# Scores in four pieces with key-projection matmuls between them, and a new order on four engines

## What is computed

```
q, k, v = split(x @ Wqkv)                      # 16 heads of 64
q, k    = l2norm(q)*qs, l2norm(k)*ks;  rotary(q, k)
out     = local_attention(q, k, v)             # windows of 32, looking one window back
x       = x + out @ Wo
x       = x + gated_gelu_ffn(layernorm(shift_tokens(x)))
```

## Time and profile before

| what | value |
|---|---|
| median of 3 runs | 1763.34 us (1762.8 to 1766.48) |
| the profiled execution's own time | 1768.14 us |
| its span in the trace | 1766.4 us |
| PE / PEld busy | 90% / 71% of the span |
| DVE / ACT / POOL busy | 77% / 72% / 73% |
| mean granted TensorE clock | 0.964 |
| the 96 `scores` groups | from 250.9 us to 1722 us, 13.5 to 19 us apart |

### The profile page before, as it was taken

One profiled execution on the slowest core, in us unless ns is written; L12 is line 12 of the kernel. 1 busy time (PEld: TensorE's weight loads), 2 busy tenths in 40 slices (PEclk: granted clock), 3 DMA queues, 4 the chain that ended last, 5 costly groups with the idle time before them and its releaser, 6 DMA issues.

```text
span 1766.4 us, 70552 instructions
## 1 busy us (share of the span) xinstructions
PE 1592.2 (90%) x29272; PEld 1260.5 (71%) x29272; DVE 1363.8 (77%) x1875; ACT 1274.8 (72%) x1888; POOL 1294.2 (73%) x1227
## 2 busy tenths in 40 slices
PE   6999968889999999999998999998989988989986
PEld 4777856667777777777776777766767766767774
DVE  5677866787887888888887878877877877877863
ACT  3788845677787778767886877777777777667663
POOL 3311168787987888888899878888877988778761
PEclk8999998999999999999999999999999999999997
DMA  5211112433334333334333343333343333333331
GB/s 150 62 47 44 44 37 63 126 87 77 94 78 107 96 86 91 86 77 128 81 94 95 77 124 81 84 83 84 76 124 72 91 81 81 72 71 77 71 75 42
DMA packets 127629, 146.51 MB, mean 83 GB/s; under 512 B 58448, under 2 KB 71504, under 8 KB 125776
## 3 DMA queue, kind: packets, MB, share of 16 engines
q1 hardware_dynamic: 127312, 141.98, 32.6%
HBM read 25.47 MB, written 1.05 MB: 15 GB/s over the span
## 4 chain that ended last, share of the span: by engine, by line
PE 70%; ACT 10%; issue 9%; DVE 4%; POOL 3%; SPq 3%; DMA 1%; ACTq 0%; POOLq 0%; DVEq 0%
PE banks L1260 41%; PE banks L1582 9%; PE banks L1542 8%; PE banks L1498 7%; PE banks L1390 4%; ACT vst L839 4%; ACT banks L854 3%; SPq L414 2%; POOL arena L631 1%; POOL arena L586 1%; POOL arena L637 1%; DMA arena<-vst 1%; DVE gq L1169 0%; DVE small L1131 0%; PE banks L1600 0%
## 5 line engine op out<-in xcount | busy, mean ns | idle before, releaser
L581 POOL TENSOR_TENSOR arena<-arena 128x1024 f32<-128x1024 f32 x96 | 230.7, 2403 | 87.8 <-DVE arena L1102 87.4
L1097 DVE TENSOR_TENSOR arena<-banks,tabs 128x1024 f32<-128x1024 f32 x192 | 233.9, 1218 | 49.5 <-PE banks L1498 26.6
L1149 DVE TENSOR_REDUCE small<-banks 128x16 f32<-128x1024 f32 x96 | 117.6, 1225 | 185.1 <-PE banks L1542 185.1
L796 ACT ACTIVATE arena<-banks 128x1024 f32<-128x1024 f32 x96 | 98.5, 1027 | 216.5 <-PE banks L1260 216.4
L839 ACT ACTIVATE vst<-banks 128x1024 f32<-128x1024 f32 x192 | 196.7, 1025 | 75.6 <-PE banks L1260 71.7
L1542 PE MATMUL banks<-arena 64*32 64x64 f32 x12288 | 162.9, 227 | 90.7 <-issue 48.9
L1102 DVE TENSOR_TENSOR arena<-banks,tabs 128x1024 f32<-128x1024 f32 x192 | 233.2, 1215 | 0.0
L586 POOL TENSOR_TENSOR arena<-arena 128x1024 f32<-128x1024 f32 x96 | 228.3, 2378 | 0.0
L1542 PEld LDWEIGHTS banks<-arena 64*32 64x32 f32 x12288 | 142.6, 106 | 104.8 <-issue 100.8
L576 POOL TENSOR_TENSOR prob<-prob,small 128x1024 f32<-128x1024 f32 x96 | 184.3, 1919 | 31.8 <-DVE small L1139 31.5
L1582 PE MATMUL banks<-arena 128*32 128x128 f32 x6144 | 198.7, 284 | 2.1 <-DVE arena L1202 1.5
(11 more groups left out here) (146 smaller groups left out, 3754.7 us busy)
## 6 DMA issues: line engine op xcount, KB each, us to landing
arena<-vst SPq DMA_DIRECT2D x1536, 64.0 KB
qkraw<-in_wqk_dram SPq DMA_DIRECT2D x6, 1024.0 KB, 6.2
arena<-in_wvo_dram SPq DMA_DIRECT2D x5, 1024.0 KB
tabs<-in_tab_dram SPq DMA_DIRECT2D x40, 128.0 KB, 2.5
gq<-w1w SPq DMA_DIRECT2D x64, 64.0 KB, 2.0
lns<-Xt SPq DMA_DIRECT2D x96, 32.0 KB
lns<-Xt SPq DMA_DIRECT2D x96, 31.8 KB
xsH<-w1w SPq DMA_DIRECT2D x32, 64.0 KB, 2.0
```

What stands on the lines that cost most here:

```text
L581: pool.tensor_tensor(kc, kc, ks, ALU.add).then_inc(s["k_add"], 1)
L1097: dve.tensor_tensor(heads(c), heads(two(0)), table(k % NT, kind), ALU.mult).then_inc(s[done], 1)
```

## The change

No matmul is added or dropped. On TensorE, `projected` makes one half (one bank, three matmuls) at a call, and `scores` is cut by pairs of columns into `scores_a` to `scores_d` (64 records each). The waits of `scores` stay at its first piece, `s_mm` is given by its last; the claim and the waits of the key projection stay at its first half, `k_mm` comes with its second.

```
@@ tensor
-            def projected(k, z):
+            def projected(k, z, h):
...
-                for h in range(2):
...
+                c0, c1 = 512 * h, 512 * (h + 1)
+                mm(bk(h), xH, qkH[:, z, c0:c1], True, False)
+                mm(bk(h), xH, qkL[:, z, c0:c1], False, False)
+                return mm(bk(h), xL, qkH[:, z, c0:c1], False, True)
...
+            def scored(k, part):
+                for j in range(2 * part, 2 * part + 2):
...
             for G in range(STEPS):
-                project_queries(G - 1)
+                project_queries_last(G - 1)
                 ln_columns(G - 6)
-                if G == 1:
-                    shifts(0)
                 transpose_queries(G - 2)
                 values_upper(G - 2)
                 next_products_lower(G - 2)
+                up_value(chunk_at(G, 12), 1)
                 up_gate(chunk_at(G, 10), 1)
-                up_value(chunk_at(G, 12), 1)
+                down_first(chunk_at(G, 13))
                 up_value(chunk_at(G, 12), 2)
+                if G == 1:
+                    shifts(0)
+                down_last(chunk_at(G, 13))
+                transpose_probs(G - 3)
                 up_gate(chunk_at(G, 10), 0)
-                down_first(chunk_at(G, 13))
-                down_last(chunk_at(G, 13))
                 up_value(chunk_at(G, 11), 0)
-                transpose_probs(G - 3)
-                scores(G - 2)
+                scores_a(G - 2)
+                scores_b(G - 2)
+                scores_c(G - 2)
+                if G:
+                    project_keys_first(G)
+                next_shifts(chunk_at(G, 12))
+                scores_d(G - 2)
                 next_products_upper(G - 2)
+                layer_columns(chunk_at(G, 13))
                 if G:
-                    project_keys(G)
+                    project_keys_last(G)
                 up_gate(chunk_at(G, 10), 2)
-                next_shifts(chunk_at(G, 12))
-                layer_columns(chunk_at(G, 13))
                 transpose_keys(G - 1)
                 weigh(G - 3)
                 values_lower(G - 1)
+                project_queries_first(G)
@@ gpsimd
             for G in range(STEPS):
-                first_steps(G)
-                shifted_lower(chunk_at(G, 15))
-                next_key_weights(G - 1)
                 refine(G - 1)
                 scale_keys(G - 1)
+                row_shifts(G - 5)
+                next_table(G - 2)
+                rotate_queries(G - 1)
+                next_query_weights(G - 1)
                 clear_lookback(G - 1)
-                row_shifts(G - 5)
-                rotate_queries(G - 1)
                 clear_values(G)
-                next_query_weights(G - 1)
+                first_steps(G)
+                next_key_weights(G)
+                shifted_lower(chunk_at(G, 14))
                 scale_queries(G - 1)
-                next_table(G - 2)
                 rotate_keys(G)
                 scale_probs(G - 2)
                 seeds(G)
@@ scalar
             for G in range(STEPS):
-                gelu(chunk_at(G, 10), 0)
-                next_query_upper(G - 1)
+                copy_layer(chunk_at(G, 13))
+                normalise_rows(G - 5)
                 if G:
                     square_keys(G)
+                shifted_upper(chunk_at(G, 13))
                 next_key_upper(G)
+                copy_keys(G - 1)
                 gelu(chunk_at(G, 10), 2)
-                copy_layer(chunk_at(G, 13))
-                shifted_upper(chunk_at(G, 13))
                 exponentials(G - 2)
-                normalise_rows(G - 5)
-                copy_keys(G - 1)
                 copy_values_lower(G - 1)
+                copy_columns(G - 5)
                 square_queries(G)
                 copy_queries_T(G - 1)
-                copy_columns(G - 5)
                 copy_values_upper(G - 1)
                 next_folded_lower(G - 1)
                 mask_scores(G - 1)
                 roots(G)
                 gelu(chunk_at(G, 9), 1)
                 copy_probs(G - 2)
-                next_w1_upper(ahead_at(G, 12))
+                next_query_upper(G)
+                gelu(chunk_at(G, 9), 0)
+                next_w1_upper(ahead_at(G, 11))
                 next_folded_upper(G - 1)
@@ vector
             for G in range(STEPS):
+                sum_keys(G - 1)
+                denominators(G - 3)
+                moments(G - 5)
+                lower_columns(G - 6)
+                next_biases(chunk_at(G, 13))
                 sum_queries(G - 1)
-                lower_columns(G - 6)
+                next_folded_lower(G - 2)
                 cosine_queries(G - 1)
                 gated(chunk_at(G, 12), 1)
+                sine_queries(G - 1)
+                gated(chunk_at(G, 12), 2)
+                gated(chunk_at(G, 11), 0)
+                next_w1_lower(ahead_at(G, 13))
+                residual(chunk_at(G, 13))
+                maxima(G - 2)
+                next_folded_upper(G - 2)
                 if G == 1:
                     biases(0)
-                sine_queries(G - 1)
-                next_folded_lower(G - 2)
-                gated(chunk_at(G, 11), 0)
-                residual(chunk_at(G, 13))
-                maxima(G - 2)
-                gated(chunk_at(G, 12), 2)
-                next_folded_upper(G - 2)
-                next_biases(chunk_at(G, 12))
                 subtract(G - 2)
-                next_w1_lower(ahead_at(G, 13))
                 if G:
                     cosine_keys(G)
                 if G:
                     sine_keys(G)
-                sum_keys(G)
                 attended(G - 3)
-                denominators(G - 2)
-                moments(G - 4)
```

More of the change, by code:

```diff
@@ L1355, in project_keys, with project_keys_last @@
                     pe.wait_ge(s["wk_L"], k // TILES + 1)
-                    projected(k, 0).then_inc(s["k_mm"], 1)
+                    claim(0, 1)
+                    projected(k, 0, 0)
                     freed[0] = freed[1] = ("k_s", k + 1)
+            def project_keys_last(k):
+                if is_tile(k):
+                    projected(k, 0, 1).then_inc(s["k_mm"], 1)
             def score_row(o, it, h, i):
@@ L1482, in _ @@
                     ("gB_cp", NSTEP) if i < 6 else ("gS_exp", NSTEP) if i == 6 else ("g_add", PAIRS)
-            project_keys(0)
+            project_keys_first(0)
+            project_keys_last(0)
             project_rows(PAIRS - 2)
@@ L1499, in transposes, with project_queries_first, project_queries_last @@
                 return ins
-            def project_queries(k):
+            def project_queries_first(k):
                 if is_tile(k):
                     pe.wait_ge(s["wq_L"], k // TILES + 1)
-                    projected(k, 1).then_inc(s["q_mm"], 1)
+                    claim(0, 1)
+                    projected(k, 1, 0)
                     freed[0] = freed[1] = ("q_s", k + 1)
+            def project_queries_last(k):
+                if is_tile(k):
+                    projected(k, 1, 1).then_inc(s["q_mm"], 1)
             def transpose_keys(k):
@@ L1530, in key_pair, with scores_a @@
                 return kT[r, j, :].rearrange("p (b t) -> p b t", b=KB)[:, KB - 1::1 - KB, :]
-            def scores(k):
+            def scored(k, part):
+                for j in range(2 * part, 2 * part + 2):
+                    for w in range(NW):
+                        for o in range(2):
+                            r = slice(64 * o, 64 * o + 64)
+                            ins = pe.matmul(bk(4 + o)[WIN * w:WIN * (w + 1), 64 * j:64 * (j + 1)],
+                                            qT[r, j, WIN * w:WIN * (w + 1)], key_pair(r, j, NW * k + w - 1),
+                                            start=False, stop=True, skip_group_check=True)
+                return ins
+            def scores_a(k):
                 if is_tile(k):
@@ L1537, in scores, with scores_b, scores_c, scores_d @@
                     pe.wait_ge(s["look"], k // NT + 1)
-                    for j in range(NP):
-                        for w in range(NW):
-                            for o in range(2):
-                                r = slice(64 * o, 64 * o + 64)
-                                ins = pe.matmul(bk(4 + o)[WIN * w:WIN * (w + 1), 64 * j:64 * (j + 1)],
-                                                qT[r, j, WIN * w:WIN * (w + 1)], key_pair(r, j, NW * k + w - 1),
-                                                start=False, stop=True, skip_group_check=True)
-                    ins.then_inc(s["s_mm"], 1)
-                    freed[4] = freed[5] = ("s_sub", k + 1)
+                    scored(k, 0)
+                    freed[4] = freed[5] = ("s_sub", k + 1)
+            def scores_b(k):
+                if is_tile(k):
+                    scored(k, 1)
+            def scores_c(k):
+                if is_tile(k):
+                    scored(k, 2)
+            def scores_d(k):
+                if is_tile(k):
```

(1 more changed line is left out.)

8 lines of the change are left out of this document (1 added, 7 removed).

## The result

The changed kernel took 1734.7 us (median of four runs, 1731.75 to 1739.99), the kernel before beside it 1764.91 us (1762.8 to 1766.71): a ratio of 0.983, with a 95% interval of 0.980 to 0.986. It is 30 us faster. The forecast was 1752, 11 us faster, with 1738 to 1760 as its own range and 1724 to 1780 as the wide one.

The account below looks back on a forecast made before the run. TensorE was taken as the bound, running out of instructions at 256-instruction block boundaries. -26.3 + 7.5 + 9 - 6 + 6 = -9.8, taken as -11 from the 1763.3 median, gave 1752 us, range 1738 to 1760.

Parts of the forecast that it names:

- the ring: Rival: the loop from scores through rotation, query projection and mask takes the 0.72 us delay whole; 1778 us, chance 0.2.
- the late gaps: 19 instruction gaps late in or just behind `scores`: each 0.72 us shorter, 9 clock lowerings fewer; -26.3 us.
- the gap vanishes: Rival: PE's queue takes in part d during the slow key matmuls, so late gaps disappear; 1716 us, chance 0.14.
- The nine earlier gaps: Instruction gaps at records 172 to 192 of `scores`, in part c: claimed to stay, no gain counted.
- Scores end later: Scores finish 0.72 us later, delaying the query projection in kind 3 (+6) and some early steps (+1.5).
- Kind 1: Kind-1 steps: `square_keys` and `sine_keys` end later, moving the query projection by 0.45 us; 20 steps, +9 us.
- Shifts: `next_biases` no longer waits for `shifts` and `w1_lower` fills DVE's idle time: 1.2 us a layer, -6 us.
- Layer ends: At layer ends on POOL, the second `qkL` comes later: 0.5 + 0.7 us a layer, +6 us, bounds -4 and +9.

Follow-up runs that it names:

- the shifted list: The kernel before with 96 satisfied waits in TensorE's list ahead of the loop over steps, so block boundaries fall 96 records earlier; 1777.18 us (one run).

## Why the prediction was right and wrong

What bounds the kernel was read rightly: TensorE runs out of instructions at block boundaries, the clock falls behind long gaps, and the ring pays for later scores. The mechanism of the gain was wrong. The forecast gave all of its gain at the gaps, 26.3 us, to the cut and nothing to the order of the work ahead of `scores`. The cut alone made the kernel 18 us slower and loses a little or nothing in the new order; the new order alone gave the whole gain (ratio 0.980, and 0.983 the second time), and one moved call of it alone as much as the whole change (0.983). That the sign came out right is luck, and 1734.7 lies outside the forecast's own range.

The step that failed is the one on the late gaps, and the error sits in one sentence: "Boundaries keep their places, since nothing is moved across the start of `scores`". That is true, and I took it to mean that the gaps' lengths could change by the cut alone. I never priced `transpose_probs` moving ahead of the gate and value groups, nor `copy_columns` and `lower_columns` moving up; both stood in the diff.

*The late gaps*, forecast -26.3 (19 x 0.72 and 9 clock lowerings). As a statement on what the cut does to gaps the step was fair: alone it took the 13 late gaps at records 193 to 252 from 31.6 to 16.0 us (12 of them), 1.1 us each where a gap was left, and the 12 behind from 17.9 to 10.2, 0.64 each. What the cut costs beside that outweighed it in the old order, 0.86 us in each clean step of kind 0 alone. But the new order started 15 of 18 late fetches ahead of S. Gaps and clock together gave 86 by the estimate above. I had a case for it, "the gap vanishes" with 1716 us and a chance of 0.14, whose reason was the wrong one (the queue taking part d in during the slow matmuls).

*The nine earlier gaps* (records 172 to 192) "lie in part c and stay". Their boundaries (records 165 to 192) had 17.9 us of pauses before and 4 to 5 after, and of six late fetches one stayed. The cut cannot reach them, so they were the quickest refutation of my step.

*Scores end later*, forecast +7.5 over kinds 3 and the early steps, with kinds 2 and 0 covered by their room. In kind 3 the profile shows the step as I read it:

```profile
878.64 0.45 PE L1546 MATMUL banks<-arena 64*32 64x64 f32 x32
879.22 1.23 DVE L1149 TENSOR_REDUCE small<-banks 128x16 f32<-128x1024 f32 x1 [1.70 <-PE banks L1546]
...
882.83 1.22 DVE L1102 TENSOR_TENSOR arena<-banks,tabs 128x1024 f32<-128x1024 f32 x1
...
884.19 0.47 PE L1260 MATMUL banks<-qkH,xsH 128*128 128x512 f32 x1
```

With S at 876.66, `maxima` starts at S+2.56 instead of S+1.87 and the query projection at S+7.53 instead of S+7.16. That is 0.37, not 0.25, and the clean kind-3 step grew by 0.49. Kinds 2 and 0, counted at nothing, grew by 0.29 and 0.36. With 22 steps each of kinds 2 and 3 and 11 of kind 0 that makes 21 us. But not all of it comes from later scores. In the new order without the cut clean steps took 14.6 (kind 2), 13.75 (kind 3) and 14.4 us (kind 0). So the cut costs kind 2 nothing, as forecast, kind 3 about 0.35 and kind 0 about 0.43, together some 12 us instead of 7.5; kind 0, counted at nothing, is most of the difference. The growth of kind 2 comes from the order: 22 of the 27 waits for L576 in the first list of waits above lie in its steps. The rival of the ring at 1778 was right in that the cut costs more than it saves.

*Kind 1*, forecast 0.45 a step, +9. Measured +0.86, 13.9 us over the 16 that had no gap before. S is 905.61 in these rows:

```profile
908.25 1.22 DVE L1149 TENSOR_REDUCE small<-banks 128x16 f32<-128x1024 f32 x1 [2.48 <-PE banks L1546]
...
910.50 1.02 ACT L796 ACTIVATE arena<-banks 128x1024 f32<-128x1024 f32 x1
...
911.61 1.23 DVE L1097 TENSOR_TENSOR arena<-banks,tabs 128x1024 f32<-128x1024 f32 x1 [0.81 <-ACT arena L796]
...
914.12 0.47 PE L1260 MATMUL banks<-qkH,xsH 128*128 128x512 f32 x1 [0.61 <-DVE arena L1102]
```

`square_keys` ends at S+5.91 (forecast 5.6) and the projection stands at S+8.51 (forecast 7.96, before 7.51). The chain is the one I named; each link was 0.2 to 0.3 us later than summed.

*Shifts*, forecast -6: the five steps took 85.4 us before and 80.1 after; clean ones 16.30 and 15.97. Of the 5.3 us only 5 x 0.33 = 1.6 are the shifts, the rest is clock and gap. *Layer ends*, forecast +6: 189.3 and 189.0 us in eleven steps, and clean 18.22 to 17.90 and 15.67 to 16.56, so +0.6 a layer, half of what I gave. But the eleven steps leave out the one just ahead of them, and there a cost lies that the prediction took for a possible gain ("the first `qkL` is ready earlier"). On POOL the first `qkL` now stands ahead of `scale_queries` in the step of tile 77, and likewise of tiles 13, 29, 45 and 61. In the changed kernel, with S at 1422.55:

```profile
1428.25 2.41 POOL L505 TENSOR_TENSOR qkL<-qkraw,qkH 128x1024 fp32r<-128x1024 f32 x1
1430.60 1.92 POOL L637 TENSOR_TENSOR arena<-arena,small 128x1024 f32<-128x1024 f32 x1
...
1432.57 0.71 PE L1501 MATMUL banks<-cst,arena 64*128 64x64 f32 x16 [0.76 <-POOL arena L637]
...
1436.81 0.71 PE L1501 MATMUL banks<-cst,prob 64*128 64x64 f32 x16 [0.52 <-POOL prob L576]
```

`scale_queries` starts at S+8.05 instead of S+6.06 as in tile 41, and TensorE waits for it and for the probabilities behind it. Tiles 13, 29 and 45, clean in both kernels, went from 13.71, 13.48 and 13.52 us to 15.07, 15.10 and 15.07, and the step is as long without the cut (15.08). That is 1.5 us a layer, some 5 us in all beyond what kind 3 is charged with above. The terms measured add up to 21 + 14 + 3 + 5 = 43 of the 56 us lost; the other 13 are not placed. Putting that `qkL` back was not tried.

The Trainium skill, "Runtime: NRT & Kernel Launch", section "Instruction fetch mechanics", calls the crossing "mostly hidden". Both kernels disagree where the block is mostly short matmuls, by 67 and 17.5 us; the shifted list (28 gaps, 26 where the count put them) agrees with its blocks of 256 instructions.

## What to carry to other kernels

Where an engine with many short instructions shows idle "issue" at equal distances in its list, look up when the instruction packet starts and what that engine waited for just ahead of the burst. The cheapest cure here was order: longer matmuls, and not short ones, as the last work ahead of the wait. Releasing earlier what the queue waits for gave 1.3% by itself but did not add to that. Price a new order step by step on every engine, also where no wait seems to be near: here it was worth more than the edit that the forecast was about. Breaking up the burst itself delays whoever needs its end, so it pays only at the tiles where a boundary falls late, and these can be counted when the program is built.

## What the runs showed of the hardware

- A fetch lasts about 1.1 us in the kernel before (median of 235 packets). Where it is late, TensorE goes on 1.2 to 1.5 us behind its end. In the ten cases in which the boundary before is crossed just behind S, the fetch starts 0.6 to 1.5 us after the crossing.
- Tile 77's block was entered at S-2.0 in both kernels; the next fetch started at S+1.85 before the change and at S-1.13 after it. The late ones all start once the wait for the mask is over. What decides between the two is open. The time at which the last wait ahead of the mask's is passed does not decide it in kinds 2 and 3 (late at S-2.0 in tile 77 before, in time at S-1.9 after), and the bytes of the value copies are excluded.
- The number of late fetches varies between profiles of the same program (3 and 5 of 32 for the order alone, gaps of 24 and 31 us). The runs of one kernel on one chip lay up to 1.3% apart (1718.57 to 1740.85 us). Single profiles of such kernels should not be compared to a few microseconds, as I did for the order alone (21 us by profile, 6 by medians).
